# A four-layer graph network on one core: GpSimd claims the row slots of the attention layer's ring 8 at a time in place of 32

## What is computed

```python
    def _L3_gnn_ref(x, edge_index, edge_weight, W, a_l, a_r, bias):
        row, col = (edge_index[0], edge_index[1])
        Wh = jnp.einsum('ni,hio->hno', x, W)
        e_l = jnp.einsum('hno,ho->hn', Wh, a_l[..., 0])
        e_r = jnp.einsum('hno,ho->hn', Wh, a_r[..., 0])
        e = e_l[:, row] + e_r[:, col]
        e = jax.nn.leaky_relu(e, negative_slope=NEG_SLOPE)
        e = e + jnp.log(jnp.clip(edge_weight, 1e-08, None))[None, :]
        eT = e.T
        e_max = jax.ops.segment_max(eT, col, num_segments=n)
        alpha = jnp.exp(eT - e_max[col])
        alpha_sum = jax.ops.segment_sum(alpha, col, num_segments=n)
        alpha = alpha / (alpha_sum[col] + 1e-08)
        msgs = alpha[:, :, None] * jnp.transpose(Wh, (1, 0, 2))[row]
        out = jax.ops.segment_sum(msgs, col, num_segments=n)
```

## Time and profile before

| | |
|---|---|
| median of 3 runs | 8844.25 us (8837.06 to 8844.64) |
| the profiled execution | 8821.84 us, span 8820.0 us |
| busy: PE, DVE, ACT, POOL | 6004.0, 3830.5, 2410.1, 1701.7 us |
| windows 0 to 23, from the first L1402 to that of window 24 | 5188.0 to 8716.0 us of the span |
| gathers of this stage (L870) | 1563, busy 1497.3 us |

### The profile page before, as it was taken

One profiled execution on the slowest core, in us unless ns is written; L12 is line 12 of the kernel. 1 busy time (PEld: TensorE's weight loads), 2 busy tenths in 40 slices (PEclk: granted clock), 3 DMA queues, 4 the chain that ended last, 5 costly groups with the idle time before them and its releaser, 6 DMA issues.

```text
span 8820.0 us, 167686 instructions
## 1 busy us (share of the span) xinstructions
PE 6004.0 (68%) x48672; PEld 5105.3 (58%) x48673; DVE 3830.5 (43%) x9102; ACT 2410.1 (27%) x7270; POOL 1701.7 (19%) x1781
## 2 busy tenths in 40 slices
PE   2777799999999789999999904343434434444346
PEld 2666687878788689999999902232222222222224
DVE  7999888888888521111122202222222222222224
ACT  3666655555555311100011101111111111111112
POOL 1000000000000100000000064444444444443430
PEclk9999999999999889999999956666666666666667
DMA  6777788888888746666666621111111111111110
GB/s 212 294 295 295 296 326 322 326 331 331 323 326 328 260 156 261 266 264 261 263 256 248 198 47 32 34 32 34 32 34 32 34 32 33 33 33 32 34 31 17
DMA packets 420634, 1542.51 MB, mean 175 GB/s; under 512 B 77499, under 2 KB 108229, under 8 KB 368588
## 3 DMA queue, kind: packets, MB, share of 16 engines
q1 hardware_dynamic: 354388, 1405.92, 42.1%
q0 software_dynamic: 58784, 129.00, 6.2%
q10 hardware_dynamic: 7186, 4.22, 0.2%
HBM read 797.39 MB, written 743.08 MB: 175 GB/s over the span
## 4 chain that ended last, share of the span: by engine, by line
PE 55%; another core or an unknown queue 18%; DVE 10%; issue 9%; ACT 3%; ACTq 2%; DMA 2%; POOL 0%; SPq 0%; DVEq 0%; POOLq 0%
PE psum L1211 20%; PE psum L1166 12%; PE psum L1458 7%; PE psum L1131 7%; PE psum L1436 5%; DVE field L1698 4%; ACT field L1081 1%; ACT field L945 1%; ACTq L931 1%; PE psum L1456 1%; DVE work L2027 1%; DVE work L2034 1%; DVE field L1691 1%; PE psum L1157 0%
## 5 line engine op out<-in xcount | busy, mean ns | idle before, releaser
L1166 PE MATMUL psum<-field 128*128 128x200 bf16 (+1 forms) x14112 | 2067.2, 273 | 54.2 <-DVE field L1698 46.0
L945 ACT COPY field<-psum x4704 | 1670.5, 417 | 1121.8 <-PE psum L1166 1020.0
L870 POOL DMA_INDIRECT field<-head_table,cmp x1563 | 1497.3, 958 | 2000.3 <-PE psum L1458 1537.6
L1211 PE MATMUL psum<-field 128*128 128x128 f32 x14406 | 1789.3, 284 | 0.0
L1211 PEld LDWEIGHTS psum<-field 128*128 128x128 f32 x14406 | 1764.7, 190 | 0.0
L1698 DVE TENSOR_TENSOR field<-field 128x1176 bf16<-128x1176 bf16 x2352 | 1651.8, 765 | 0.0
L1456 PE MATMUL psum<-zero_b 128*128 128x2 bf16 x1611 | 289.8, 180 | 1717.8 <-ACT field L1081 1303.1
L1456 PEld LDWEIGHTS psum<-zero_b 128*128 128x128 bf16 x1611 | 171.9, 107 | 1894.0 <-issue 1873.9
L1166 PEld LDWEIGHTS psum<-field 128*128 128x128 bf16 x14112 | 1056.6, 99 | 337.7 <-issue 57.1
L1081 ACT COPY field<-psum x1611 | 433.6, 269 | 2784.1 <-remote 1629.5
L2084 DVE TENSOR_SCALAR params<-iota,cmp 128x128 f32<-128x128 f32 x1616 | 340.6, 286 | 1510.1 <-PE psum L1458 1170.5
(11 more groups left out here) (316 smaller groups left out, 3740.9 us busy)
## 6 DMA issues: line engine op xcount, KB each, us to landing
adj<-field SPq DMA_DIRECT2D x1764, 400.0 KB, 4.1
field<-adj SPq DMA_DIRECT2D x294, 1600.0 KB
X<-adj SPq DMA_DIRECT2D x49, 1600.0 KB, 7.6
work<-adj SPq DMA_DIRECT2D x49, 1600.0 KB, 7.6
field<-head_table,cmp POOLq DMA_INDIRECT x1563
field<-in_edge_attr SPq DMA_DIRECT2D x4, 3072.0 KB, 23.8
head_table<-field ACTq DMA_DIRECT2D x49, 68.0 KB, 1.6
tile_rows<-field SPq DMA_DIRECT2D x1, 3328.0 KB, 19.1
```

The source lines that it names most:

```text
L870: pool.indirect_dma_start(out=rows3[:, (i * WIN + t) * ROW3:(i * WIN + t + 1) * ROW3], out_offset=None, in_=head_table, in_offset=bass.Ind ...
L945: act.copy(evac[:, :, bass.ds(place, HALF)], build_banks[:, bass.ds(bank, NSEG * SEG)].rearrange("p (w c) -> p w c", w=ARRAYS)).then_inc(p ...
L1166: mm = pe.matmul(build_banks[:, bass.ds(cur[j % ROUND], end - first)], hot, pr[:, first:end], start=False, stop=True, skip_group_check=True)
L1211: mm = pe.matmul(ps_y[slot], source[:, hi, :], adj_in[slot][h].rearrange("p (g c) -> p g c", c=HALF)[:, :, at:at + 2], start=(hi == 0), st ...
```

## The change

```diff
--- before.py
+++ after.py
@@ -91,7 +91,7 @@
 TAB_KINDS = 3
 T_SRC, T_CARRY, T_PLACE = range(TAB_KINDS)
 SUB = 8
-CLAIM = 32
+CLAIM = 8
 HOTS = 2
 assert ROUNDS3 * DEPTH == WINDOWS - 1 and HALVES * WIN == P and TCOLS3 * P >= WINDOWS * WIN
 assert (TCOLS3 * HALVES - 1) * WEDGES + WSLOTS + 2 <= min(PADN, RIGHT_N + 2)
```

## The result

The changed kernel takes 8227.0 us in the median of 4 runs (8214.89 to 8236.25), the kernel before 8844.44 (4 runs beside them). The ratio is 0.9303, with a 95% interval of 0.9292 to 0.9314: 7.0% faster. The forecast was 8160, the range 7940 to 8580. The profiled execution took 8214.89 us, 606.95 less than that of before.

What follows compares the result with a forecast made beforehand. No engine was full: bursts of gathers held back TensorE's counts, 77.3 us per window. 21 windows save 651 us, with windows 0 and 22 685, so 8821.8 gives 8136; the median lies 22 above: 8160 us, range 7940 to 8580.

Steps and rivals of the forecast that it cites:

- The hold: In the last stage, a burst of gathers holds TensorE's counts back 1.41 us per gather; all pass at its end.
- The cycle, (b): Short burst of 8 gathers in the steps: 0.78 us to start plus 11.3 us hold, taken as 12.3 us.
- Rival 1: Slower: the free start is not renewed between short bursts; cycles of 17.2 us, 9095 us in all; chance 0.12.
- The number of bursts, (b): Seven short bursts of 8 gathers in each window's steps, 5.9 us each, 41.3 us together.
- The head, (c): One short burst in the next window's softmax head costs 5 us, bounds 0 and 13; head about 22 us.
- The sum of a window: Windows 1 to 21 of the last stage: 71.4 + 41.3 + 5 = 117.7 us each, 31.0 less than before.
- Window 0 and 22, (d): First window and the one gathering only 27 rows: regrouped bursts change them by -13 and -21 us.
- Rival 5: Claims start late, after VectorE's comparisons end: a short burst costs 6.9 us, 8315 us in all; chance 0.04.
- Rival 3: The free start comes back in part: cycle 14.5 us, head 8 us, 8565 us in all; chance 0.17.
- rival 4: More than forecast: a short burst costs 4.5 us, the head 0, 7835 us in all; chance 0.06.
- Rival 2: No change: gathers do not hold TensorE or cost the same however grouped; window 148.7 us, 8850 us; chance 0.04.
- The signs: Changed profile: ScalarE's longest remote wait under 10 us, POOL's L1458 wait some 800, head about 22, window 23 at 71.

Runs made afterwards that it cites:

- the later claims: The changed kernel (CLAIM = 8) with each claim waiting for nine more steps, so none falls in the softmax head: 8196.22 us, ratio 0.9273.
- the run without the seam: The kernel before (CLAIM = 32) with the seam matmuls (L1436) only in the last window, seam sums left out elsewhere: 8686.76 us, one run.

## Why the prediction came out as it did

The likeliest case held: the cost sits in long bursts, and short ones cost less. Point by point:

- *The hold.* 1.41 us a gather was forecast; bursts of 8 and 16 give 1.45 (11.6 and 23.2 us in the mean of 54 and 61 bursts). All held counts have passed at its end. Right.
- *The cycle, (b).* 12.3 us forecast, 12.3 to 12.4 measured, in the changed kernel and six times a window with the later claims. Rival 1, a cycle of 17 us, falls.
- *The number of bursts, (b).* This step failed. I forecast seven bursts of 8 and let the next claim be opened by the end of the hold, as if TensorE had done none of its 8 steps when a burst begins. Its lead grows through bursts of 8, though, until up to two of the eight are copied at the start and the rest 4.2 to 7.3 us later (in the 27 that follow a burst of 8). Then the next claim is open before GpSimd has issued 8 gathers, and the two become 16. A burst of 16 costs 28.8 us for 16 steps, 4.0 more than two of 8. At 1.6 a window that is 6.5 us.
- *The head, (c).* 5 us were forecast for one burst of 8 and a head of 22. The head is 16.8 (16.4 to 17.3 in windows 1 to 21), but the burst is one of 16, since the claim of step -8 waits for the table of indices, which I had passed over. I had looked at GpSimd's wait for row_added alone. The next burst comes 28.9 us later, and without gathers the rest of the head and 8 steps take 16.8 - 3.3 + 6.4 = 19.9: it costs 9.0.
- *The sum of a window.* 71.4, six bursts of 8 at 12.4 - 6.4 = 6.0, 9.0 for the head's, 6.5 for the merged: 122.9 worked out afterwards, 121.8 measured, 117.7 forecast. Two errors nearly cancel in it: one burst fewer in the steps is 6.0 us less, the head's burst costs 4.0 more. So the forecast's nearness to the time is in part luck; the cycle, on which most of it rests, is not. 21 times the 4.1 us are 86 us, and with 2 for window 22 and 9 the other way from the earlier start they make the 79 us between 8136 and 8214.9.
- *Window 0 and 22, (d).* -13 and -21 forecast, -13.4 and -18.7 measured.
- *Rival 5,* a claim that waits for VectorE's comparisons, would give a near time, 8315, but its cycle would be 6.4 + 6.9 = 13.3 us, and it is 12.4. *Rival 3*, a cycle of 14.5, and *rival 4*, bursts that cost 4.5 us and a head that costs nothing, fall with the same 12.4. *Rival 2,* that the gathers cost the same however grouped, falls with every run above.
- *The signs.* POOL's waits were forecast at some 800 us for L1458; they are 452.2 for L1458, and the 374.9 for the table, which I had not forecast, bring them near it by chance, to 827. ScalarE's longest wait was to be under 10 us and is 18.2: the burst of 16. The head was to take about 22 us and takes 16.8. Window 23 stays, as forecast.

## What stays open

Between 1.44 and 1.58 us the pace alone makes a difference (472 us of late counts, then none); between 1.26 and 1.44 a fill and a wait came with it. Plain transfers show that it is the indirect gathers, but not which of their three differences. What takes 1.41 us a gather was not found. Half rows and half bytes exclude that it scales with either, and the packets show that it is not the transfer. How much TensorE does in a hold was not settled: the run without the seam speaks against a fixed number of steps, and no fixed number of matmuls fits it. Why its lead grows when the claims lie at every eighth step, and hardly does when they lie nine steps later, is open too. Whether TensorE's matmuls themselves come late, or only their counts, the traces can't tell, since matmul ends are modelled. A claim that waits for nothing but row_added, with two tables of indices in turn, wasn't tried, nor a spacing between 1.44 and 1.58 us.

## What to carry to other kernels

When a stage is slow and no engine is full, divide its time by what runs beside it: a window with 64 gathers, one with 27 and one with none gave the price of a burst before anything was changed. Then ask what a producer does to the counts of the others while it works ahead of need: here the slots came free early, and to fill them at once with indirect gathers was the fault (plain transfers did no harm), so a small delay after each gather gained more (11%) than the finer claims (7%). And where a claim is made smaller, look at everything the claiming engine waits for, and at whether the consumer gets a little further ahead in each cycle; once it opens the next claim before the burst is over, the bursts grow together again.

## What was not expected of the hardware

- Indirect gathers issued on GpSimd each 1.26 us delay what waits for TensorE's counts by up to 31.9 us; at 1.44 us apart the longest is 8.4, and at 1.58 none shows.
- The delay goes by the gather, 1.41 us, for 128 rows of 544 bytes, 64 rows of 544 and 128 rows of 272. Plain transfers of the same size on the same queue, 0.53 us apart, show none.
- The data of the gathers is not late: through the whole burst of 32 its packets start 1.6 to 1.7 us after each gather, and the counts of TensorE stay held for 3.9 us after the last packet.
- A gather of 64 rows takes 0.91 us to issue, one of 128 rows 0.95: nearly all of it is fixed, by these two sizes.
- The granted clock goes with the gaps: in the steps of window 10 at 1.58 us spacing TensorE is busy for 50.2 of 57.5 us and the clock is 0.87, nearer the upper of its two levels (1.2 and 2.4 GHz, 0.50 and 1.00); in a burst before it is busy for 7.2 of 11.3 us at 0.69, and then for 4.8 of 33.8 at 0.55.
